# Fourteen rounding copies a batch on GpSimd in place of ScalarE, in a four-layer graph attention kernel

## The reference

```
h   = inp @ W;  e[i,j] = leaky_relu(h[i] @ a1 + h[j] @ a2);  e = -inf where adj == 0
out = softmax(e) @ h
```

## Time and profile before

| | |
|---|---|
| time, median of 3 runs | 2834.45 us (2833.2 to 2836.31) |
| the profiled execution | 2838.34 us, its span 2836.5 us |
| mean granted TensorE clock | 0.994 of full speed |
| PE, DVE, ACT, POOL busy | 98%, 87%, 80%, 23% |

### The profile page before, as it was taken

One profiled execution on the slowest core, in us unless ns is written; L12 is line 12 of the kernel. 1 busy time (PEld: TensorE's weight loads), 2 busy tenths in 40 slices (PEclk: granted clock), 3 DMA queues, 4 the chain that ended last, 5 costly groups with the idle time before them and its releaser, 6 DMA issues.

```text
span 2836.5 us, 63430 instructions
## 1 busy us (share of the span) xinstructions
PE 2793.0 (98%) x23704; PEld 2492.5 (88%) x23704; DVE 2454.7 (87%) x6405; ACT 2281.5 (80%) x6079; POOL 648.3 (23%) x1051
## 2 busy tenths in 40 slices
PE   7999999999999999999999999999999999999996
PEld 7888889888998898898898888889988989888885
DVE  6898888898888988888988888988889888889875
ACT  5788878888878888888888788788788888887785
POOL 4122122221122221122221122221122211222111
PEclk9999999999999999999999999999999999999998
DMA  2000000000000000000000000000000000000000
GB/s 83 9 9 9 16 16 16 16 1 17 16 16 17 16 2 16 16 16 16 8 9 16 16 16 16 1 16 16 16 16 16 2 16 16 16 16 9 2 9 15
DMA packets 16785, 41.83 MB, mean 15 GB/s; under 512 B 5344, under 2 KB 7392, under 8 KB 16480
## 3 DMA queue, kind: packets, MB, share of 16 engines
q1 hardware_dynamic: 16480, 37.77, 3.8%
HBM read 20.99 MB, written 16.78 MB: 13 GB/s over the span
## 4 chain that ended last, share of the span: by engine, by line
PE 92%; DVE 5%; ACT 2%; issue 1%; SPq 0%; DMA 0%; POOL 0%; POOLq 0%; DVEq 0%
PE bank L597 48%; PE bank L695 23%; PE bank L729 8%; PE bank L683 4%; PE bank L647 4%; PE bank L816 1%; PE bank L671 1%; DVE R L920 1%; PE bank L767 1%; DVE Z L1015 1%; PE bank L773 1%; DVE oTlo L1021 0%; DVE R L1006 0%; PE bank L706 0%; DVE hT2lo L878 0%
## 5 line engine op out<-in xcount | busy, mean ns | idle before, releaser
L695 PE MATMUL bank<-hw,R 128*128 128x257 f32 x3072 | 722.0, 383 | 1.4 <-ACT hw L1241 1.2
L695 PEld LDWEIGHTS bank<-hw,R 128*128 128x128 f32 x3072 | 565.4, 191 | 86.9 <-issue 8.3
L1422 POOL TENSOR_TENSOR rs<-ve,mhalf 128x4 f32<-128x4 f32 x128 | 140.6, 1098 | 1830.2 <-DVE ve L863 1746.1
L920 DVE SCALAR_TENSOR_TENSOR R<-bank,E,mask_ne 128x512 f32<-128x512 f32 x640 | 452.3, 743 | 3.0 <-PE bank L683 2.2
L597 PE MATMUL bank<-wfc_hi,oThi 128*128 128x256 f32 (+1 forms) x1024 | 298.8, 292 | 0.0
L597 PE MATMUL bank<-wfc_hi,oTlo 128*128 128x256 f32 (+1 forms) x1024 | 288.5, 282 | 0.0
L597 PE MATMUL bank<-wfc_lo,oThi 128*128 128x256 f32 (+1 forms) x1024 | 288.5, 282 | 0.0
L729 PEld LDWEIGHTS bank<-hw,R 128*64 128x64 f32 x8192 | 251.0, 138 | 32.4 <-issue 29.2
L729 PE MATMUL bank<-hw,R 128*64 128x65 f32 x8192 | 269.0, 224 | 0.1
L1220 ACT ACTIVATE Z<-bank,rs 128x258 f32<-128x258 f32 (+1 forms) x384 | 176.0, 478 | 47.4 <-PE bank L597 46.5
L597 PEld LDWEIGHTS bank<-wfc_hi,oThi 128*128 128x128 f32 x1024 | 194.1, 190 | 1.0
(11 more groups left out here) (293 smaller groups left out, 8415.1 us busy)
## 6 DMA issues: line engine op xcount, KB each, us to landing
x<-in_x_dram SPq DMA_DIRECT2D x32, 512.0 KB, 3.6
out_dram<-x SPq DMA_DIRECT2D x31, 512.0 KB, 2.6
R<-in_adj_dram SPq DMA_DIRECT2D x2, 512.0 KB, 7.6
Z<-in_L_gnn_mlp_w_dram SPq DMA_DIRECT2D x2, 512.0 KB, 5.6
O<-in_L_gnn_W_fc_dram SPq DMA_DIRECT2D x1, 1024.0 KB, 7.1
out_dram<-x SPq DMA_DIRECT2D x4, 128.0 KB, 1.8
R<-in_L_gnn_W_dram SPq DMA_DIRECT2D x1, 256.0 KB, 4.0
R<-in_L_gnn_W_hand_dram SPq DMA_DIRECT2D x1, 256.0 KB, 6.6
```

Source lines behind the costliest of these rows:

```text
L695: ins = e.matmul(bk[:, 0:257], P[:, j, i * 128:(i + 1) * 128], hw[:, j, 0:257], start=(j == 0), stop=(j == NBLK - 1))
L920: e.scalar_tensor_tensor(P[:, t, :], bank_of(b, "row", p)[:, :], m["E"][:, 1, h, j:j + 1], mask[:, j, :], ALU.max, ALU.mult).then_inc(up(" ...
L1422: e.tensor_tensor(m["rs" + z][:, :], m["ve" + z][:, :], mhalf[:, :], ALU.pow).then_inc(up("rs", b), 1 if l == 1 else 3)
```

## The change

The 14 copies are taken out of `scalar_batch` and put in `pool_batch`, as `tensor_copy` in place of `copy`, with the same waits, operands and semaphores. In POOL's generator they stand between `power(e, w, b, 1)` and `presum(2, 0)`, in the order o1, Phi, o2, o3. ACT's generator keeps all else in its order. One step of ACT's for o1 (activation and copy) is now one step with the activation alone, and the same for o3; the 8 steps of Phi and o2 are gone.

The first line of POOL's string and of TensorE's, and the code:

```diff
     "pe": (
-        "www00ww0000w000w00ww01ww010ww01111ww1wwwwww11ww00w110000100100100002002100000000000000000020200021102000001011"
+        "wwww00ww00w000000011w0w0ww011101ww1wwwwwwwwww0011w000011000010000100122000001000000000000020220002002011000101"
...
     "pool": (
-        "wwwwwwwwwwwwwww0wwwwwwwww1wwww000000w000ww00000000000000001111112111111111111111111122222232222222222222222222"
+        "wwwwwwwwwwwwwww0wwwwwwww0w000wwwwwww00000000100000010000011101111110001001000011000000112111111122221222211212"
...
@@ -1274,8 +1275,6 @@
             for fo in range(4):
                 w.wait_ge(*at("m1", b, fo))
                 e.activation(O1[:, fo, :], bank_of(b, "m1", fo)[:, :], ACT.Relu, bias=b1[:, fo:fo + 1]).then_inc(up("m1a", b))
-                w.wait_ge(*at("m1a", b, fo))
-                e.copy(oT["hi"][:, fo, :], O1[:, fo, :]).then_inc(up("o1hi", b))
                 yield
             for n in range(NBLK):
                 w.wait_ge(*at("h", b, 1, n))
@@ -1296,15 +1295,8 @@
                 e.copy(HB[s]["hi"][:, n, :], bank_of(b, "hs2", n)[:, 0:F]).then_inc(up("hB", b))
                 yield
 
-            for n in range(3):
+            for n in range(4):
                 yield from high_hB(n)
-            for j in range(NBLK):
-                if j == 1:
-                    yield from high_hB(3)
-                w.wait_ge(*at("hs2", b, 3))
-                w.wait_ge(*at("P", b, 4, j))
-                e.copy(oT["hi"][:, j, :], R[s][:, j, :]).then_inc(up("Phi", b))
-                yield
 
             def exf(u):
                 return (R[s][:, 4, :], rowt[s][:, :])[u % 2]
@@ -1323,11 +1315,6 @@
                 e.activation(exf(u), exf(u), ACT.Exp, bias=minus1[:, 0:1]).then_inc(up("ef", b))
                 yield
 
-            def high_o2(u):
-                w.wait_ge(*at("o2", b, u))
-                e.copy(Rr[s][:, u, :], O1[:, (u + 2) % 4, :]).then_inc(up("o2hi", b))
-                yield
-
             w.wait_ge(*at("dn", b, 1))
             w.wait_ge(*at("Plo", b, 3))
             e.copy(R[s][:, 3, :], bank_of(b, "dn")[:, :]).then_inc(up("rDr", b))
@@ -1335,17 +1322,12 @@
             for u in range(4):
                 yield from elus(u)
                 yield from again(u)
-                if u:
-                    yield from high_o2(u - 1)
-            yield from high_o2(3)
 
 
             for fo in range(2):
                 ta = Z[s][:, fo * 512:(fo + 1) * 512]
                 w.wait_ge(*at("m2", b, fo))
                 e.activation(ta, bank_of(b, "m2", fo)[:, :], ACT.Relu, bias=b2[:, fo:fo + 1]).then_inc(up("m2a", b))
-                w.wait_ge(*at("m2a", b, fo))
-                e.copy(hT[s]["hi"][:, fo, :], ta).then_inc(up("o3hi", b))
                 yield
             for bp in range(2):
                 w.wait_ge(*at("r3", b, bp))
@@ -1453,6 +1435,23 @@
                     yield
 
             yield from power(e, w, b, 1)
+            for j in range(NBLK):
+                w.wait_ge(*at("m1a", b, j))
+                e.tensor_copy(oT["hi"][:, j, :], O1[:, j, :]).then_inc(up("o1hi", b))
+                yield
+            for j in range(NBLK):
+                w.wait_ge(*at("hs2", b, 3))
+                w.wait_ge(*at("P", b, 4, j))
+                e.tensor_copy(oT["hi"][:, j, :], R[s][:, j, :]).then_inc(up("Phi", b))
+                yield
+            for u in range(4):
+                w.wait_ge(*at("o2", b, u))
+                e.tensor_copy(Rr[s][:, u, :], O1[:, (u + 2) % 4, :]).then_inc(up("o2hi", b))
+                yield
+            for fo in range(2):
+                w.wait_ge(*at("m2a", b, fo))
+                e.tensor_copy(hT[s]["hi"][:, fo, :], Z[s][:, fo * 512:(fo + 1) * 512]).then_inc(up("o3hi", b))
+                yield
             yield from presum(2, 0)
             yield from power(e, w, b, 2)
             yield from power(e, w, b, 3)
```

More of the change, by code:

```diff
@@ L80 @@
[L80 to L84, removed]
@@ new lines @@
+        "01120000000012111211110102120000110111021101100000011111111102012100001101101111000000100112231122111122312223"
+        "23322211322311113312121111111222223222222221313322223111212121321112211222212123314222223223332433334433323324"
+        "32222432343234242232232234333343332334334234222232323433332332222232325333344333444435444455444434354333354345"
+        "43454333333354444454444544445334533533434345444444333333433455644454544455645556566555446556444454564644444445"
+        "55556555555566564455556444454554565454445555445454665755555656665766667766656566755755675665665557755565676666"
@@ new lines @@
+        "76665666677567556556657656665665555565658666677666777768777788777677687668667867767876666666877777877778778776"
+        "67887666676768777777666666676788977787877788978889899888779889777787897977777778888898788888899879888897777878"
+        "8789887778888777878799a888889988998a9999aa99989899a88a889a89989988a88a88989a9999999999a9aa889a88988998a9989989"
+        "988888989899b99aa999aaaa9baaaabbaaaa9a9ba9999ba9aba9aba9999999baaaaabaaaababaaa99abba9999a9a9baaaaaa9999999a9a"
+        "bbcaaababaaabbcabbbcbccbbbaacbbcaaaababcacaaaaaaabbbbbbcbbbbbabccbacbbbbcaaaababbabcabbaabbbbaaababaccdbbbbcbb"
@@ new lines @@
+        "cbccbdccccddcccbcbccdbbdbbcdbccbccdbbbbdbbcbcdcccccbdccccccddbcdbbcbbccbdcbcccbccbbbbbcbcbeccccddcccddddcedddd"
+        "eeddddcdcedccccedcdedcdedcccccccedddddeddddeecddddcdeedccccdcdceddddddcccccccdcdeefdddededddeefdeeefeffeeeddfe"
+        "efddddeddeffdddddddeeeeefeeeeeeefdfedfeeeefddddedeedefeedddeeeedddededffgeeeeeeeffffegffffggfffefeffgeegeefgef"
+        "feffgeeeegeefefgffffffffegfffggefgeefeeffegffeffeffeeeeefefehffffggfffggggfhgggghhggggfgfhgffffhgfghgfghgfffff"
+        "ffhggggghgggghgggghffghhgffffgfgfhggggggffffffgffghhiggghhgggghhighhhihiihhhggihhigggghgiighggggggghhhhhihhhhh"
@@ new lines @@
+        "hhiigihhhghhigggghghhghihhgghghhhggghghgihijhhhhhhiiiihjiiiijjiiihihiijhhjhhijhiihiijhhhhjhhihijiiiiijiiiiiijh"
+        "jhijhhihhiihjihiiihiihhhhhihihkiiiijiijijjjjikjjjjkkjjjjijikjiiiikjijkjijkjiiiiiiikjjjjjkjjjjkjjjjkiijkkjiiiij"
+        "ijikjjjjjjiiiiiiijijkkljjjkjkjjjkkljkkklkllkkkjjlkkljjjjkjkjlljjjjjjjkkkkklkkkkkljklkklkkjkkljjjjkjkkjklkkjjjk"
+        "kkkjjjkjkjllmkkkkkkkllllkmllllmmlllklkllmkkmkklmkllkllkmkkkmkklklmlllllllmllllmkmklmkklkkllkmlklllkllkkkkklklk"
+        "nllllmmlllmmmmlnmmmmnnmmmmlmlnmllllnmlmnmlmnmlllllllnmmmmmnmmmmnmmmmnllmnnmllllmlmlnmmmmmmlllllllmlmnnommmnmnm"
@@ new lines @@
+        "mmnnomnnnonoonnnmmonnommmmnmnomommmmmmmnnnnnonnnnnnnoomnmonnnnommmmnmnnmnomnnmmnnnnmmmnmnmoopnnnnnoonnoonpoooo"
+        "ppooononoponnpnnopnoonoopnnpnnnnonopooooooopoooopnpnopnnonnoonpoonoonoonnnnnononooqooppoooppppoqppppqqppppopoq"
+        "pooooqpopqpopqpoooooooqpppppqppppqppppqoopqqpoooopopoqppppppooooooopopqqrpppqpqpppqqrpqqqrqrrqqqpprqqppprpqpqr"
+        "prpppppppqqqqqqrqqqqqqrrpqprqqqqrppppqpqqpqrqqpppqqqqpppqpqprrsqqqqqqqrrrrsqrrrrssrrqrrqsrrqqsqqsrqrrsqsrqrqqq"
+        "qqqrsrrrrsrsqrrrrsrrqrsrqqqqrqrqrsrrrrqrrqqqqqrqrqtrrrrssrrsrsssrtssssttssssrsrsrrrrttrsstrsstsrrrrrrrststssss"
```

201 lines of the change are left out of this document (91 added, 110 removed).

## The result

The changed kernel takes 2919.9 us (median of 4 runs, 2913.9 to 2920.3), the kernel before 2834.65 us: a ratio of 1.030, with a 95% interval of 1.028 to 1.031. That is 85 us, or 2.7 us a batch, slower. I had forecast 2836 us and a range to 2857.

A forecast was written before the change was run, and what follows sets the result against it. TensorE, busy 98%, was taken as the bound. 2836.5 + 0 (fill) + 3.2 (middle) - 1.5 (drain) = 2838.2, plus 1.8 around it = 2840.0; the runs' median lies 3.9 lower, so 2836 us, range 2825 to 2857.

The forecast's parts named there:

- ACT's and POOL's sums: Whole run: ACT loses 273 us of copies, POOL gains 314 us at 0.70 us a copy; POOL not a bound.
- o1 at no cost: o1 stage, 4 copies a batch: POOL's copy runs beside ACT's next activation and meets no subtraction; cost 0.
- the DVE time in the o2 stage: o2 stage: four subtractions 0.05 us longer each, 0.2 us a batch, half reaching TensorE; 3.2 us over 32 batches.
- Phi at no cost: Phi stage, 4 copies a batch: a chain of 3.5 to 5.5 us, covered by TensorE's other work; priced at 0.
- o3 as a gain of room: o3 stage, 2 copies: second copy ends at 2.06 us instead of 2.60; 0.5 us of room, 0 in the middle.
- rival a: o2 stage: contended POOL copies of 1.25 us overfill the stretch, 0.6 us late a batch, 19 us, 2853; chance 0.2.
- Rival (c): Whole run: 448 subtractions 0.05 us longer add 22 us to DVE, still 87%; moves nothing alone; chance included in rival a.
- The new turns at no cost: o1 and Phi stages: TensorE work between stages 1.3 us (2.0 before) and 4.6 (4.7 before); cost 0.
- Fill and drain at 0 and -1.5: Run's ends: fill 0 +- 7 us for clock changes; drain -1.5 us, half of 3.2 us idle TensorE from 2700 to 2765.

The follow-up runs named there:

- e7: Kernel before with its old turns, only the 4 o1 copies a batch moved to POOL: 2839.1 us, +3.
- e9: Kernel before with its old turns, only the 4 o2 copies a batch moved to POOL: 2858.6 us, +24.
- e11: Kernel before, POOL untouched, with an extra 128x160 DVE copy ahead of each of the 14 subtractions a batch: 2875.3 us, +41.
- e3: Kernel before plus 14 extra 128x512 reading copies a batch on POOL that nobody waits for: 2899.9 us, +65.
- e1: Kernel before with all 14 copies a batch moved to POOL, DVE's and TensorE's turns as before: 2906.0 us, +71.
- e8: Kernel before with its old turns, only the 4 Phi copies a batch moved to POOL: 2860.0 us, +24.
- e10: Kernel before with its old turns, only the 2 o3 copies a batch moved to POOL: 2849.8 us, +15.
- e6: Changed kernel with its 14 POOL copies a batch replaced by memsets of the same destinations, which read nothing: 2861.7 us, +26 over the kernel before.
- e4: As e3, but each extra POOL operation is a memset of the spare 128x512 tile, which reads nothing: 2838.6 us, +4.
- e12: As e3, but the 14 extra POOL copies a batch moved beside DVE's mask operations, which read PSUM: 2867.9 us, +33.
- e5: e1 with its 14 POOL copies a batch replaced by memsets of the same destinations: 2845.8 us, +10 over the kernel before.
- e14: e6 with the memsets of o1, Phi and o3 cut to 4 columns, o2's whole: 2856.9 us, +23 over the kernel before.
- e13: e5 with the memsets of o1, Phi and o3 cut to 4 columns, o2's whole: 2840.3 us, +6.5 over the kernel before.
- e2: Changed kernel's new DVE and TensorE turns, with the 14 copies a batch put back on ACT: 2928.1 us, +93 over the kernel before.

## Why the prediction was wrong

**ACT's and POOL's sums: right.** ACT fell by 216 us (273 forecast; instructions overlap in the trace, so busy time moves less than the sum of their lengths, which fell by 274), POOL rose by 365 (314), a copy alone is 0.61 us.

**o1 at no cost: right in the time**, by e7 (+3 us), but in part by luck. I had the copies meet no subtraction, and in e7 DVE loses 15 us: the subtraction of L997 (L999 there) has a mean of 719 ns, 688 before. In this stage little of it reached TensorE.

**The term that failed is the DVE time in the o2 stage,** "0.05 us for each of four subtractions, 0.2 us a batch" and "half of it reaching TensorE". The mechanism was named and its sign was right; the size was wrong, and the other stages had it at nothing. For the o2 stage alone e9 measured 0.5 us of DVE time a batch (17/32) in place of 0.2, and 24 us of the time in place of 3.2. For all stages POOL's reading takes 68 to 70 us of DVE's time, 2.1 to 2.2 us a batch, and 59 to 61 us of the time. Three faults made it. I counted one operation only, line 1049, where every operation with two SBUF inputs that meets a copy counts: lines 1015, 1021 and 997 rose by 70 to 121 ns, and operations of other stages and batches too. I took the excess from its mean over operations of which few met anything, and not from the one that did, the 967 ns: 0.28 us for one meeting was in the trace. And I let half of it reach TensorE in the one stage where DVE was full, not everywhere; e11 gives 0.6 for DVE time that is merely added, e3 gives 65/81 = 0.8, e1 71/74, and e9 more than one, since POOL's late copies are in it.

**Phi at no cost: wrong**, by e8 (+24 us). I asked whether the copies would be in time, and they are. I did not ask what they do to DVE, which makes the additions just then.

**o3 as a gain of room: wrong**, by e10 (+15 us). I counted the room that the faster chain gives and not what the copies meet. What they meet is known in part. The subtractions of L1071 stay long with memsets in the place of the copies (846 ns in e6 in the lane that has 892 in the changed kernel, 690 before), so most of their lengthening there comes from other operations of POOL, above all the steps of a presum, which stand beside o3's copies in POOL's turns. In e10 L897's mean is up as well (306 ns, 266 before). How the 15 us divide between the copies and a presum that they push later was not tried.

**The rule of the Trainium skill.** The Trainium skill, page "SBUF — State Buffer" (section "Who interferes with whom"), says that a VectorE instruction with two SBUF inputs contends with a GpSimd instruction that reads SBUF, and not with one that only writes. e3 against e4 shows both halves (+65 us and +4). I quoted the rule, and then used its full price for POOL's lateness alone (rival a), with 0.05 us for DVE. Either of the two can lose, and the one that counted most was DVE. The Trainium skill calls the shared port in the same section "an exclusive lock", so a meeting would cost up to a whole operation of the other. The longest copy of e12, 1200 ns in place of 617, is within that, as a subtraction takes 684.

**Rival (a), POOL as a queue (2853): not the mechanism.** With POOL's queue and hand-over but no reading, e5 costs 10 us. The sign that I named for it, more than 10 us of matmul waits on lines 1021 or 1049, did not show (0.8 us from 150 to 2760 us, all on L1050), while TensorE's idle time, to stay under 10 us, was 53.8. **Rival (c), DVE as the bound, came nearest,** and I set it aside on DVE's share of the span, 87%, with "by itself it moves nothing". Its share was 87% before and 87% after; only the chain told the difference.

**The new turns at no cost: wrong**, by e14 against e13 (about 17 us). With o1 at 3, Phi at 24, o2 at 24 and o3 at 15 us, that makes 83 of the 85 us. I compared how much TensorE work lay between the stages and found it alike, which says nothing of DVE's order. That e2 costs 93 us is explained only in part: ACT's waits are seen, but how they add to the turns' own cost was not tried.

**Fill and drain at 0 and -1.5: near.** Their idle time moved by +1.6 and -1.6 us. The lower clock of the last 72 us (0.79, 0.86 before) was not in the forecast, and 0.07 x 72 = 5 us more of missing clock outweigh the 1.6 us.

## What to carry to other kernels

In this kernel copies moved to a half-idle GpSimd were paid for by VectorE, when they read SBUF while VectorE ran operations with two SBUF inputs: count those operations over the whole stretch, price each meeting by the longest instance in the trace and not by a mean, and put the copies beside VectorE's PSUM reads or leave them on ScalarE. Reading operations that GpSimd already had (here the presums) collide too when a new order brings them beside VectorE's. An engine at 87% in a pipeline with thin slack can be a second bound: ask what one more microsecond of it does, whatever the first bound's share is.

## What the runs showed of the hardware

- A 128x512 float32 rounding copy takes 0.61 us on GpSimd alone, the same as 0.62 on ScalarE; under VectorE's two-input operations its median is 1.07 us (Phi), at most 1.20 (e12).
- A memset of the same tile takes 0.53 us on GpSimd and disturbs VectorE by 3 us over 448 of them; 448 reading copies of the same tile disturb it by 81 us, 0.18 us each (e3, e4).
- VectorE operations with one tensor input and columns of SBUF as the other operands are held up too: a 128x512 one took 729 ns beside a GpSimd copy and 538 otherwise (e12), a 128x4 one about 500 ns beside GpSimd's additions and 223 otherwise. Operations with one input from PSUM kept their 740 ns beside the copies.
